# Rows scaled by ScalarE in four buffers ahead of GpSimd's scatter, in a cross-attention and expert-layer kernel on one core

## The reference, cut to what matters

```python
x = x + L0_xattn(layernorm(x), ctx)        # attention over the 120 context rows
x = x + L0_ffn(layernorm(x))               # shared expert + one routed expert of eight
x = x + L1_xattn(layernorm(x), ctx, ctx)
x = x + L1_ffn(layernorm(x))               # eight decision trees

def L0_ffn(x):
    logits = x @ gate_w                    # 8 experts
    top_val, top_id = max(logits), argmax(logits)
    xs = x * sigmoid(top_val)              # each row scaled by its own score
    y[e] = (silu(xs @ rt_gate[e]) * (xs @ rt_up[e])) @ rt_down[e]
    return swiglu_shared(x) + y[top_id]
```

## Time and profile before

| | |
|---|---|
| median of 3 runs | 884.05 us (882.87 to 887.5) |
| time of the profiled execution | 888.12 us |
| its span in the profile | 886.3 us |
| granted TensorE clock, mean | 0.979 of full speed |
| busy: TensorE, its weight loads, VectorE, ScalarE, GpSimd | 92%, 69%, 74%, 60%, 28% |

### The profile page before, as it was taken

One profiled execution on the slowest core, in us unless ns is written; L12 is line 12 of the kernel. 1 busy time (PEld: TensorE's weight loads), 2 busy tenths in 40 slices (PEclk: granted clock), 3 DMA queues, 4 the chain that ended last, 5 costly groups with the idle time before them and its releaser, 6 DMA issues.

```text
span 886.3 us, 14989 instructions
## 1 busy us (share of the span) xinstructions
PE 817.5 (92%) x4208; PEld 615.1 (69%) x4249; DVE 651.5 (74%) x1701; ACT 535.7 (60%) x931; POOL 250.6 (28%) x328
## 2 busy tenths in 40 slices
PE   4899998887689979999999999999999999999997
PEld 3677776675566656767777777777777777777775
DVE  4578778876564325577888888888888888889774
ACT  2365565644333323436677768776877777777765
POOL 1112111167817744211132223212321332131000
PEclk9899999999889989999999999999999999999999
DMA  5225674553234433210000000000000000000000
GB/s 144 58 82 149 177 208 129 166 139 112 69 95 130 142 98 104 84 49 24 13 25 25 1 24 24 24 0 24 24 24 0 24 24 21 3 24 13 13 1 24
DMA packets 91422, 55.66 MB, mean 63 GB/s; under 512 B 13440, under 2 KB 88184, under 8 KB 91256
## 3 DMA queue, kind: packets, MB, share of 16 engines
q1 hardware_dynamic: 74304, 40.38, 16.1%
q0 software_dynamic: 4096, 8.40, 3.3%
q10 hardware_dynamic: 12983, 6.41, 2.6%
HBM read 32.10 MB, written 23.07 MB: 62 GB/s over the span
## 4 chain that ended last, share of the span: by engine, by line
PE 32%; DVE 24%; issue 15%; POOL 14%; ACT 10%; DMA 2%; DVEq 1%; another core or an unknown queue 1%; POOLq 0%; ACTq 0%; SPq 0%
POOL x_sorted L502 6%; PE PS L746 5%; POOL rs L487 4%; DVE sil_l L1398 4%; DVE dec L1382 3%; PE PS L764 3%; DVE xn_c L1078 3%; DVE st L1067 3%; PE PS L997 3%; PE PS L999 3%; PE PS L998 3%; ACT sil L703 2%; PE PS L1019 2%; PE PS L1021 2%; PE PS L1020 2%
## 5 line engine op out<-in xcount | busy, mean ns | idle before, releaser
L703 ACT ACTIVATE sil<-PS,b_in_c 128x512 f32<-128x512 f32 x256 | 162.2, 685 | 113.3 <-PE PS L1006 72.0
L1398 DVE TENSOR_TENSOR sil_l<-sil,sil_h 128x512 fp32r<-128x512 f32 x256 | 164.7, 685 | 44.6 <-ACT sil_h L711 43.8
L485 POOL TENSOR_TENSOR ve<-mv,eps 128x4 f32<-128x4 f32 x64 | 17.5, 273 | 499.5 <-DVE mv L1072 499.5
L711 ACT ACTIVATE sil_h<-sil 128x512 fp32r<-128x512 f32 x224 | 128.9, 631 | 0.0
L1019 PE MATMUL PS<-sil_h,wout_l 128*128 128x512 f32 x256 | 117.9, 460 | 1.6 <-DVE sil_l L1398 1.6
L1382 DVE TENSOR_SCALAR dec<-PS,b_in_c 128x512 bf16<-128x512 f32 x128 | 95.5, 746 | 25.3 <-PE PS L999 23.5
L997 PE MATMUL PS<-x4T_h,win_l 128*128 128x512 f32 x256 | 102.4, 400 | 1.6 <-ACT yo L663 0.7
L1021 PE MATMUL PS<-sil_h,wout_h 128*128 128x512 f32 x256 | 100.6, 393 | 0.0
L1020 PE MATMUL PS<-sil_l,wout_h 128*128 128x512 f32 x256 | 100.2, 391 | 0.0
L999 PE MATMUL PS<-x4T_h,win_h 128*128 128x512 f32 x256 | 99.8, 390 | 0.0
L998 PE MATMUL PS<-x4T_l,win_h 128*128 128x512 f32 x256 | 99.8, 390 | 0.0
(11 more groups left out here) (153 smaller groups left out, 1593.9 us busy)
## 6 DMA issues: line engine op xcount, KB each, us to landing
x_sorted<-zeros SPq DMA_DIRECT2D x4, 1280.0 KB, 7.2
xs_in<-x_sorted SPq DMA_DIRECT2D x20, 256.0 KB
y_sorted<-yo ACTq DMA_DIRECT2D x20, 256.0 KB
X<-in_x SPq DMA_DIRECT2D x16, 256.0 KB
rows<-xn SPq DMA_DIRECT2D x16, 256.0 KB
xs<-rows SPq DMA_DIRECT2D x16, 256.0 KB
out<-res SPq DMA_DIRECT2D x16, 256.0 KB
ctxT<-in_ctx_t SPq DMA_DIRECT2D x16, 240.0 KB
```

Source lines behind the costliest of these rows:

```text
L703: act.activation(tile(sil[p % 2], c, W), bank(2 * (p % 2) + c), ACT.Silu, bias=b_in_c[:, 2 * p + c:2 * p + c + 1]).then_inc(t_silu, 1)
L711: act.activation(tile(sil_h[p % 2], c, W), tile(sil[p % 2], c, W), ACT.Copy).then_inc(t_hi, 1)
L1398: dve.tensor_tensor(tile(sil_l[p % 2], c, W), tile(sil[p % 2], c, W), tile(sil_h[p % 2], c, W).bitcast(F32), ALU.subtract).then_inc(t_lo, 1)
```

## The change

What it does:

- There are four buffers `xs` instead of two, in a part of SBUF that the trees' weights fill later, and `load_rows` runs up to four units ahead. In phase A units 0 to 3 are loaded at group 8, units 4 and 5 at group 14, units 6 and 7 at group 15.
- The scaling moves from GpSimd to ScalarE: four activations of 128 columns per unit, in place, the score as a per-partition scale. In phase A they stand at the start of a body; those of units 8 to 15 stand behind the scores and in bodies 0 to 6 of phase R.
- GpSimd only issues the four indirect DMAs of a unit, and reads the positions where they are.
- Loops over units on SyncE and GpSimd, and ScalarE's loop over blocks 1 to 10 of phase R, are written out.

```diff
@@ constants, buffers
+XB = 4
-        sco = sb("sco", [P, 2, G])
+        xs = [cut.take(f"xs{i}", W) for i in range(XB)]
-        xs = cut.two("xs", W)
@@ SyncE
-            def load_rows(k, v, i):
-
-                if not below(i, 1):
+            def load_rows(k):
+
+                v, i = k % XB, k // XB
+                if i:
                     sp.wait_ge(scattered[v], 16 * G * i)
                 sp.wait_ge(a_rows, 16 * (k + 1))
...
                 if g == HG:
-                    load_rows(0, 0, 0)
-                    load_rows(1, 1, 0)
-                if g > HG + 4:
-                    i = g - HG - 4
-                    load_rows(2 * i, 0, i)
-                    load_rows(2 * i + 1, 1, i)
+                    for k in range(XB):
+                        load_rows(k)
+                if g > HG + 5:
+                    for k in range(2 * (g - HG - 4), 2 * (g - HG - 4) + 2):
+                        load_rows(k)
...
-            load_rows(HG, 0, HG // 2)
-            load_rows(HG + 1, 1, HG // 2)
-            for u in range(2):
-                r_next(u, u, 0)
-            with sp.Fori(0, HR // 2 - 2) as i:
-                for u in range(2):
-                    r_next(2 * i + 2 + u, u, 0)
-                    load_rows(HG + 2 + 2 * i + u, u, HG // 2 + 1 + i)
+            for k in range(HG, HG + XB):
+                load_rows(k)
+            for r in range(HR - 2):
+                r_next(r, r % 2, 0)
+                if r > 0 and HG + XB + r - 1 < NG:
+                    load_rows(HG + XB + r - 1)
+            all_scattered(sp, NG)
@@ GpSimd
-            def scale_rows(k, v, i):
-
-                pool.wait_ge(k_in[v], 16 * (i + 1))
-                pool.tensor_copy(idx[:, v, :], cols(POS, k * G, G))
-                pool.tensor_copy(sco[:, v, :], cols(SCORE, k * G, G)).then_inc(k_idx, 1)
-                pool.wait_ge(k_idx, k + 1)
-                pool.tensor_tensor(by_tile(xs[v]), by_tile(xs[v]),
-                                   sco[:, v, :].unsqueeze(2).to_broadcast([P, G, P]), ALU.mult).then_inc(k_scaled, 1)
-
-            def scatter(k, v, h):
+            def scatter(k, h):
+                v = k % XB
                 pool.wait_ge(k_scaled, k + 1)
                 pool.sem_inc(pool_passed, 1)
                 for j in range(G):
-                    pool.indirect_dma_start(x_sorted[h], bass.IndirectOffsetOnAxis(ap=idx[:, v, j:j + 1], axis=0),
+                    at = k * G + j
+                    pool.indirect_dma_start(x_sorted[h], bass.IndirectOffsetOnAxis(ap=POS[:, at:at + 1], axis=0),
                                             tile(xs[v], j), None).then_inc(scattered[v], 16)
...
-                        pool.wait_ge(scored, 1)
-                    scale_rows(units[0], 0, units[0] // 2)
-                    scatter(units[0], 0, 0)
-                    scale_rows(units[1], 1, units[0] // 2)
+                    scatter(units[0], 0)
                 if g is not None:
                     rstd(1, g, a_mv2, a_ve2, a_rs2)
                 if units:
-                    scatter(units[1], 1, 0)
+                    scatter(units[1], 0)
@@ ScalarE
+            def scale_rows(k):
+
+                v = k % XB
+                act.wait_ge(k_in[v], 16 * (k // XB + 1))
+                act.wait_ge(scored, k // HG + 1)
+                for j in range(G):
+                    at = k * G + j
+                    i = act.activation(tile(xs[v], j), tile(xs[v], j), ACT.Identity, scale=SCORE[:, at:at + 1])
+                i.then_inc(k_scaled, 1)
...
             def a_body(f, g, l, m, u, units=(), route=None):
+                for k in units:
+                    scale_rows(k)
                 if l is not None:
                     act.wait_ge(a_x2T_ps, l + 1)
...
+                if route == "all":
+                    scale_rows(HG)
...
                 r_silu(2 * r + 1, 1)
+                if r < HG - 1:
+                    scale_rows(HG + 1 + r)
                 if not first(r):
                     r_evac_y(r - 1, 1 - u, stores, 1 if isinstance(r, int) and r > HR else 0)
 
-            r_body(0, 0, None)
-            with act.Fori(0, HR // 2) as i:
-                r_body(2 * i + 1, 1, i)
-                r_body(2 * i + 2, 0, i)
-            for r in range(HR + 1, NR):
+            for r in range(NR):
                 r_body(r, r % 2, (r - 1) // 2)
```

More of the change, by code:

```diff
@@ L178, in program @@
         cut = Cut(WORK, ARENA)
-        xs = cut.two("xs", W)
-        scatter_end = cut.at
+        scatter_end = cut.at + 2 * W
+        cut = Cut(scatter_end, ARENA)
         ctx_rows = cut.two("ctx_rows", W, KEYS)
@@ L257, in program @@
                              "dve_passed", "pool_passed"))
-        k_idx, k_scaled, k_in, scattered = sem("k_idx"), sem("k_scaled"), sems("k_in", 2), sems("scattered", 2)
+        k_scaled, k_in, scattered = sem("k_scaled"), sems("k_in", XB), sems("scattered", XB)
         r_in, r_out = sems("r_in", 2), sems("r_out", 2)
@@ L286, in slots, with all_scattered @@
             return tensors[h][bass.ds((r - h * HR) * W, W), :].rearrange("(t p) d -> p t d", p=P)
+        def all_scattered(eng, units):
+            for v in range(XB):
+                eng.wait_ge(scattered[v], 16 * G * len(range(v, units, XB)))
         def first(g):
@@ L442, in r_next @@
                 r_load(r + 2, u, h)
-            for u in range(2):
-                sp.wait_ge(scattered[u], 16 * G * (HG // 2))
+            all_scattered(sp, HG)
             sp.wait_ge(a_pv_ps, NG)
@@ L448, in _ @@
             r_load(1, 1, 0)
-            load_rows(HG, 0, HG // 2)
-            load_rows(HG + 1, 1, HG // 2)
-            for u in range(2):
-                r_next(u, u, 0)
-            with sp.Fori(0, HR // 2 - 2) as i:
-                for u in range(2):
-                    r_next(2 * i + 2 + u, u, 0)
-                    load_rows(HG + 2 + 2 * i + u, u, HG // 2 + 1 + i)
-            for u in range(2):
-                sp.wait_ge(scattered[u], 16 * G * (NG // 2))
+            for k in range(HG, HG + XB):
[5 more added lines that the diff above has]
+            all_scattered(sp, NG)
             with sp.Fori(HR // 2 - 1, NR // 2 - 1) as i:
@@ L518, in a_body @@
                 if units:
-                    scatter(units[1], 1, 0)
+                    scatter(units[1], 0)
             phase_a(a_body, pool)
             pool.wait_ge(placed, 2)
-            pool.wait_ge(scored, 2)
-            with pool.Fori(0, HG // 2) as i:
-                for v in range(2):
-                    k = 2 * i + HG + v
-                    scale_rows(k, v, HG // 2 + i)
-                    scatter(k, v, 1)
+            for k in range(HG, NG):
+                scatter(k, 1)
             def gather(h, u, half):
@@ L540, in gather @@
                                             ).then_inc(y_in[u], 16)
-            for u in range(2):
-                pool.wait_ge(scattered[u], 16 * G * (NG // 2))
+            all_scattered(pool, NG)
             for u in range(2):
```

2 lines of the change are left out of this document (1 added, 1 removed).

## The result

The change made the kernel slower: **896.22 us** median of four runs (894.25 to 899.54), against 885.23 us for the kernel before run beside it (882.87 to 887.5); ratio **1.0129**, 95% interval 1.0095 to 1.0164. The profiled execution took 895.26 us, with a span of 893.3 us.

What follows compares the result with a forecast made beforehand. GpSimd was taken as the bound in the sorting bodies and, at 7.11 us per unit, of phase R's pace. Phase A +2.4 and phase R -9.4 give -7.0 us, so 884.05 becomes 877.0 us; 8-in-10 range 872 to 884.

Steps and rivals of the forecast that it cites:

- the pace of 7.08 us ... becomes 6.53: Phase R, blocks 4 to 11: pace per block drops to 6.53 us and block 10's wait goes, 9.4 us won.
- GpSimd idle between units 8 to 15: Second half of the sorting: a sign the profile would show if the forecast was right; no size given.
- no row names the wait: Phase R: the 7.08 us block pace was taken for GpSimd's 7.11 us per unit; if not, 2.8 us less won.
- The wait of ScalarE in bodies 15 and 16: Phase A: scaling waits for late loads of units 4 to 7; bodies take 18.4 us, phase A ends 2.4 us later.
- some 4 us: Bodies 15 and 16: expected wait of ScalarE's scaling activations for the loads; wrong if under 2 us or above 8.
- Bodies 13 and 14: Phase A: first root gains 1.1 us, then a body of 13.1 + 1.0 us; next root at 206.15, 3.3 us won.
- if the loads were there ... 6.2 us earlier: Bound for phase A: with units 4 to 7 loaded in time, bodies 15 and 16 lose nothing and it ends 6.2 us earlier.
- block 10: Phase R: TensorE's 5.00 us standstill for this block, loaded only behind the last scatter, would go.
- ScalarE's scaling in the blocks costs nothing: Phase R, bodies 1 to 6: 1.2 us of scaling before `yo` costs nothing, 0.4 us to spare; at worst 0.3 us per body.
- the written-out loops: Loops written out on the engines were costed at nothing.
- VectorE beside GpSimd: Phase A: `xn`, 1.89 us beside GpSimd's multiplication, falls to 1.1 us, 0.8 us per body; otherwise 1.6 us worse.
- Rival 4: Slower: ScalarE's wait for units 4 to 7 grows, TensorE at half clock; 7.0 us more per body, 891 us; chance 0.07.

Runs made afterwards that it cites:

- e1: Changed kernel plus two unused 128x4 roots (about 2.3 us) on GpSimd ahead of each unit's scatter from unit 9 on; 891.45 us, ratio 1.0099.
- e2_early_load: Changed kernel with SyncE's loads of units 4 to 7 each a body earlier, ahead of its waits for `xn2`; 883.79 us, ratio 0.9998.
- g3: Changed kernel with loads of units 4 to 7 a body earlier and two 128x4 copies behind each indirect DMA from unit 8 on; 871.3 us, ratio 0.9835.
- f4: Changed kernel with loads of units 4 to 7 a body earlier and one GpSimd root ahead of units 10, 12 and 14 alone; 882.83 us, ratio 0.9982.
- i1: The changed kernel, unaltered, run again on chip E; 898.31 us, ratio 1.0136.
- i2: The program of e2_early_load (changed kernel with loads of units 4 to 7 a body earlier) run again on chip E; 883.53 us, ratio 0.9985.
- e3: Changed kernel where GpSimd, ahead of each unit from 9 on, waits idle until the unit before has landed (about 2.2 us); 890.48 us, ratio 1.0069.

## Why the prediction was wrong

It said 877.0 us, faster; it is 896.2. By the trace, from the root of `xn` 13 on, it forecast 7 us less and there are 8.6 more (5.6 in the bodies, 0.4 behind them, 2.6 in the blocks); the medians differ by 11.0, with 8.4 to 14.5 in the interval. The 15.6 us between forecast and trace are two steps and 0.4.

1. **The step that failed: "the pace of 7.08 us ... becomes 6.53" and "GpSimd idle between units 8 to 15", 9.4 us won.** The gain itself was right: wherever no signal was held, blocks 0 to 11 took 74.0 to 74.6 us, 9.4 to 10.0 less than before. What was missing is what the removed work did: copies and multiplication were the only pause between bursts of four DMAs. I counted the units' pitch and not how many units lay ready. By the time the positions came, units 8 and 9 were scaled, unit 10 was by 272.9, long before its turn at 279.7, and twelve DMAs went out at 1.265 us each. TensorE's signals came up to 9.7 us late, and with the low clock behind it, that cost (295.73 - 270.69) - 2 x 6.53 = **12.0 us**. None of my rivals had it. The kernel before showed a small form of it, which I took for GpSimd's pace as such: blocks 5 to 9 were copied 0.9 to 1.0 us behind the end of each burst, 0.6 to 0.8 us after TensorE had turned them, and e1 has GpSimd's pitch of 7.07 us with blocks 6.71 us apart. I had written that "no row names the wait", and went on.

2. **The wait of ScalarE in bodies 15 and 16: right in kind, 2.3 us too small.** I had 18.4 us for each body. Measured, SyncE issues the loads 3.1 us after the root, as forecast; `xn2T_h` starts 8.5 and 9.3 us after it (forecast 8.6), and the next root 10.7 us behind that (forecast 9.8). From the issue of the loads to ScalarE's start it was 3.0 us in body 15 and 3.8 in body 16 (forecast 3.2), and eight activations took 2.44 us (forecast 2.34). The rows give ScalarE 7.20 and 8.00 us of waiting, where I had written "some 4 us". Bodies 13 and 14 were 0.9 us longer than forecast. Together 3.2 us. The bound, "if the loads were there ... 6.2 us earlier", came out at 7.1 us in e2_early_load.

3. **Right: block 10.** Its wait of 5.00 us went. **Nearly right: ScalarE's scaling in the blocks costs nothing.** In g3 the steps with four activations in them are 6.53 to 6.93 us, 6.63 in the mean, and those without 6.53 to 6.54; every second one is the longer, which I have not explained. **Right: the written-out loops**, 885.18 against 884.16 us, within the interval.

4. **Right: VectorE beside GpSimd.** `xn`, 1.89 us in the earlier trace rows, takes 1.15 at the same place (198.97) now that GpSimd doesn't multiply beside it: 0.74 us come back. The Trainium skill, "GPSIMD Engine Reference", section 1, names a two-port mode or two SBUF inputs as the conditions for contention. `xn` has one large SBUF input, so the rows agree with the page only if it ran in a two-port mode, and no run here shows in which mode it ran.

Rival 4 has the right sign and the place of the smaller error. Of its 14 us for the two bodies 2.3 came true. Its half clock is there in part, as these stretches of bodies 15 and 16 show (0.87 and 0.75 of full speed behind each wait, where the kernel before had 1.00 from 209 to 225 us and 0.85 from 225 to 240); how many of the 2.3 us are the clock's I can't say.

```profile
211.50:225.00 13.50, 9.96 (x54) 8.27 (x54) 6.66 (x22) 10.21 (x24) 5.82 (x9) 0.87 0.12 42
...
231.50:245.00 13.50, 7.15 (x32) 5.85 (x32) 4.95 (x17) 8.48 (x21) 4.19 (x6) 0.75 0.07 25
```

## What to carry to other kernels

Before you take work off an engine that issues DMAs, ask what that work spaced out, and how many issues will stand ready behind each other when it is gone: count the longest run, not the mean pace. When two engines that wait for the same producer go on at the same instant, long after the producer was done, look for what a third engine was doing until a moment before. And compare kernels on one chip: two runs here pointed to a mechanism until the same program behaved otherwise elsewhere.

## What the runs showed of the hardware

While GpSimd issued indirect DMAs without a pause, completion signals of TensorE reached ScalarE, SyncE and VectorE late. With one each 1.265 us, twelve in a row held a signal for 9.5 to 9.7 us (after, e2, f4, i1, i2, on three chips at least) and let it go 2.2 to 2.4 us after the last, with 1.4 us in f4, whose twelve have a root in them; an earlier signal came 5.5 us late in the middle of the burst (after). Behind four in a row signals came about 0.95 us after the last, 0.6 to 0.8 us late in the kernel before. Spaced 1.345 us nothing improved. At 1.46 us signals were not late on chip C, and 1.1 to 2.3 us late on D and E, with the same program on C and E. At 1.57 us there was none on C and F. With 2.2 us or more between sets of four (e1, e3, and the kernel before) no block was more than 0.8 us late. An estimated need of about 1.43 us per DMA fits the releases on chips A, B and E; it doesn't fit the late signals at 1.46 us on E, nor the one in mid-burst. It is not the landing of the rows that the signals wait for: in e3_drain GpSimd itself waits for that, and it comes 2.1 to 2.6 us after the last of four, more than a us behind the 0.95. The row is GpSimd's first issue behind such a wait:

```profile
290.98 0.96 POOL L497 DMA_INDIRECT x_sorted<-xs,POS  x1 [2.14 <-DMA x_sorted<-xs,POS]
```

What it is that holds the signals, and why only TensorE's were seen to be held, was not tried, and stays open.
